# A two-layer graph network on one core: degrees counted in two halves inside the histogram, table rows begun there

## What is computed

```python
h = maximum(layernorm(x), 0)
# two graph convolutions over the edges plus one self loop per node
deg  = segment_sum(1, dst)                 # a count for each node, loop included
dinv = rsqrt(deg)
h = relu(segment_sum((h @ W)[src] * dinv[src] * dinv[dst], dst) + b)    # twice, W_pre ahead of W1
x = x + h @ W_post + b_post
h = maximum(layernorm(x), 0)
x = x + attention(h)                       # 4 heads; softmax over the heads; first N edges only
```

## Time and profile before

| | |
|---|---|
| median of 3 runs | 4163.26 us (4160.58 to 4163.69) |
| the profiled execution | 4164.72 us, its span 4163.0 us |
| busy | PE 3188.7 us (77%), DVE 1329.3 (32%), ACT 383.8 (9%), POOL 3026.6 (73%) |
| DMA | 514.10 MB, mean 123 GB/s |
| granted TensorE clock, mean | 0.825 |

### The profile page before, as it was taken

One profiled execution on the slowest core, in us unless ns is written; L12 is line 12 of the kernel. 1 busy time (PEld: TensorE's weight loads), 2 busy tenths in 40 slices (PEclk: granted clock), 3 DMA queues, 4 the chain that ended last, 5 costly groups with the idle time before them and its releaser, 6 DMA issues.

```text
span 4163.0 us, 38689 instructions
## 1 busy us (share of the span) xinstructions
PE 3188.7 (77%) x12023; PEld 1996.3 (48%) x12023; DVE 1329.3 (32%) x2800; ACT 383.8 (9%) x1055; POOL 3026.6 (73%) x3173
## 2 busy tenths in 40 slices
PE   5587787778788788787777777777777777777777
PEld 5344444444444444444444555544445555545566
DVE  6322222222222222222222333332224444434456
ACT  5100000000000000000001110111101111011112
POOL 2677777777777777777767777777777777777772
PEclk8677767777877877777778899999989899999987
DMA  7644444444444444444434444443334444444455
GB/s 228 153 121 116 121 115 121 118 118 121 116 121 118 118 121 115 121 118 119 121 99 120 118 118 121 118 118 111 113 115 118 118 118 118 118 121 126 119 163 153
DMA packets 248749, 514.10 MB, mean 123 GB/s; under 512 B 62491, under 2 KB 141832, under 8 KB 248296
## 3 DMA queue, kind: packets, MB, share of 16 engines
q0 software_dynamic: 150048, 410.73, 35.6%
q1 hardware_dynamic: 98504, 100.82, 8.3%
HBM read 471.70 MB, written 39.64 MB: 123 GB/s over the span
## 4 chain that ended last, share of the span: by engine, by line
POOL 67%; issue 22%; PE 5%; DMA 3%; DVE 1%; ACT 1%; POOLq 0%; SPq 0%; DVEq 0%
POOL sb_big L897 66%; DMA sb_big<-T,sb_srci 3%; PE bank L1181 3%; PE bank L541 1%; ACT sb_big L744 1%; PE bank L1658 0%; DMA T<-sb_big 0%; PE bank L1643 0%; POOLq L891 0%; DVE sb_big L1762 0%; PE bank L1107 0%; PE bank L1108 0%; DVE sb_big L791 0%; DVE sb_big L1709 0%; DMA sb_work<-dstT 0%
## 5 line engine op out<-in xcount | busy, mean ns | idle before, releaser
L897 POOL DMA_INDIRECT sb_big<-T,sb_srci x3126 | 2960.1, 947 | 982.5 <-issue 939.5
L1181 PE MATMUL bank<-sb_big 128*128 (+2 forms) x7056 | 2680.3, 490 | 862.2 <-DMA sb_big<-T,sb_srci 803.0
L1181 PEld LDWEIGHTS bank<-sb_big 128*128 128x128 f32 x7056 | 1382.2, 229 | 1908.6 <-issue 1759.6
L958 DVE TENSOR_TENSOR sb_work<-bank,sb_work 128x257 f32<-128x257 f32 (+1 forms) x196 | 83.4, 425 | 1609.2 <-PE bank L1181 1609.2
L945 DVE TENSOR_TENSOR sb_big<-bank,sb_win 128x2304 f32<-128x2304 f32 x196 | 501.2, 2557 | 6.7
L1011 ACT COPY sb_work<-bank 128x256 f32<-128x256 f32 x196 | 73.0, 373 | 1815.4 <-PE bank L1070 1815.4
L981 DVE SCALAR_TENSOR_TENSOR sb_work<-bank,sb_dinv,sb_b 128x256 f32<-128x256 f32 x98 | 47.4, 484 | 508.7 <-PE bank L1108 508.7
L991 DVE TENSOR_TENSOR sb_X<-sb_X,bank 128x256 f32<-128x256 f32 x98 | 41.2, 421 | 384.4 <-PE bank L1121 384.4
L1069 PE MATMUL bank<-sb_ident,sb_work 128*128 128x128 f32 x392 | 122.0, 311 | 20.3 <-DVE sb_work L981 14.3
L1070 PE MATMUL bank<-sb_ident,sb_work 128*128 128x128 f32 x392 | 120.5, 307 | 0.0
L1048 ACT COPY sb_work<-bank 128x256 f32<-128x256 f32 x98 | 36.5, 373 | 817.2 <-PE bank L1070 817.2
(11 more groups left out here) (192 smaller groups left out, 1712.5 us busy)
## 6 DMA issues: line engine op xcount, KB each, us to landing
sb_big<-T,sb_srci POOLq DMA_INDIRECT x3126, 2.8
T<-sb_big SPq DMA_DIRECT2D x14, 899.5 KB, 8.2
sb_work<-T SPq DMA_DIRECT2D x49, 257.0 KB
T<-sb_work SPq DMA_DIRECT2D x49, 256.0 KB, 2.3
sb_work<-T SPq DMA_DIRECT2D x49, 256.0 KB
sb_X<-x SPq DMA_DIRECT2D x13, 896.0 KB, 11.0
out<-sb_X SPq DMA_DIRECT2D x9, 1024.0 KB
sb_looks<-LO SPq DMA_DIRECT2D x23, 256.0 KB
```

Source lines behind the costliest of these rows:

```text
L897: pool.indirect_dma_start(out, None, table, bass.IndirectOffsetOnAxis(idx, 0)).then_inc(s.g[u % NSEM], 16)
L958: v.tensor_tensor(t.Y[:, b, 0:w], ps.A[b][:, 0:w], t.self[:, b, 0:w], ALU.add).then_inc(s.Y, 1)
L1181: mm = pe.matmul(ps.A[b][:, 0:w], t.S[:, b * K + k, :], rhs, start=(k == 0), stop=(k == K - 1))
```

## The change

It does six things. (1) The degrees are finished in two halves, tiles 0 to 62 and 63 to 97 (`HALF`): the first set of eight matmuls stands on PE behind chunk 3 (`HALF_CHUNK`), the second behind the histogram. (2) `dve_scales` of batch 0 and DVE's tiles of group 0 stand on DVE ahead of the last chunk of one-hot slices. (3) The statistics move: groups 3, 4, 5 lie between one-hot slices on DVE; ACT takes groups 7 and 8 from DVE as well, group 7 ahead of the table, group 8 between the table's groups 2 and 3, where ACT's last two evacuations stand too (`act_counted`). (4) The table has eight places for groups instead of six (`STAGES`): two in `sb_work`, six in `sb_big`, taken from its end; POOL and ACT wait ahead of group 3 for the whole histogram. (5) One-hot buffers lie elsewhere, with one of its own for the last chunk. (6) Since `sb_work` is needed early, the next destinations are loaded behind group 3 of x instead of behind all of x, and the count of unsorted ones moves from the check to the histogram (`dve_given`). Work of the same size is otherwise kept: 14 stores, 70 ACT tiles. The general path, which these inputs don't take, is adapted.

The core of the diff:

```diff
-ACT_STATS = (0, 1, 2, 6)
+ACT_STATS = (0, 1, 2, 6, 7, 8)
+HALF = 63
+HALF_CHUNK, COUNTED = 3, 3
+STAGES = 8
+STAGE_SLOT = (None, None, 36, 29, 22, 15, 8, 1)
...
+    staged, _ = take(work, 0, [2, GROUP * TW])
+    t.stage = [staged[:, k, :].rearrange("p (j d) -> p j d", d=TW) for k in range(2)]
+    t.stage += [t.ring[:, k:k + GROUP, :] for k in STAGE_SLOT[2:]]
...
         if g == 3:
...
+            sp.dma_start(t.dstn, a.dstN).then_inc(s.dstn, 16)
     sp.wait_ge(s.dve0, ZERO_X)
     sp.dma_start(t.X[0:LAST, NT - 1, :], a.x[(NT - 1) * P:N, :]).then_inc(s.x97, 16)
-    sp.dma_start(t.dstn, a.dstN).then_inc(s.dstn, 16)
...
+def pe_degrees(pe, t, s, ps, h):
+    c0, c1, out = degree_half(ps, h)
+    d = t.deg.rearrange("p (j q) -> p q j", q=8)
+    for q in range(8):
+        mm = pe.matmul(out, t.Eq[0:32, q, :], d[0:32, q, c0:c1], start=(q == 0), stop=(q == 7))
+    mm.then_inc(s.pe0, 1)
...
         if c < NOH - 1:
             mm.then_inc(s.hist, 1)
+        if c == HALF_CHUNK:
+            pe.wait_ge(s.eq, 16)
+            pe.wait_ge(s.odd, 2)
+            pe_degrees(pe, t, s, ps, 0)
     pe.wait_ge(s.odd, 4)
+    pe_degrees(pe, t, s, ps, 1)
...
-    act_stats(act, ch, t, s, 0)
-    act_stats(act, ch, t, s, 1)
+    for g in ACT_STATS[0:3]:
+        act_stats(act, ch, t, s, g)
+    ch.sync()
+    act.sem_inc(s.ast, 1)
     act.wait_ge(s.par, 16)
     act_evacuate(act, t, s, ps, 0)
-    act_stats(act, ch, t, s, 2)
...
+    for g in ACT_STATS[3:5]:
+        act_stats(act, ch, t, s, g)
+    act_evacuate(act, t, s, ps, 1)
+    act_table1(act, t, s, 0, ch, ps)
...
+        if r == 0 and g == COUNTED:
+            pool.wait_ge(s.hb, 4)
...
+def act_counted(act, ch, t, s, ps):
+    act_stats(act, ch, t, s, ACT_STATS[5])
+    ch.sync()
+    act.sem_inc(s.ast, 1)
+    act_evacuate(act, t, s, ps, 2)
+    act_evacuate(act, t, s, ps, 3)
...
+        if r == 0 and g == COUNTED:
+            act_counted(act, ch, t, s, ps)
...
         ins.then_inc(s.chunk, 1)
...
+        if c == 2:
+            dve_stats(v, t, s, 3)
+            dve_stats(v, t, s, 4)
+        elif c == 3:
+            dve_stats(v, t, s, 5)
+            dve_odd(v, t, s, ps, 0)
+        elif c == 4:
+            dve_given(v, ch, t, s)
+            dve_variance(v, ch, t, *BATCHES[0])
+            dve_sums(v, ch, t, s, 0)
+            dve_odd(v, t, s, ps, 1)
+            dve_degrees(v, ch, t, s, ps, 0)
+            dve_scales(v, ch, t, s, 0, 0)
+            dve_table1(v, ch, t, s, 0, 0, 1)
+    dve_table1(v, ch, t, s, 0, 1, 3)
     dve_stats(v, t, s, 9)
     ch.step(dve_stats(v, t, s, 10))
     dve_variance(v, ch, t, *BATCHES[1])
+    dve_odd(v, t, s, ps, 2)
+    dve_odd(v, t, s, ps, 3)
     dve_sums(v, ch, t, s, 1)
+    dve_table1(v, ch, t, s, 0, 3, 4)
+    dve_degrees(v, ch, t, s, ps, 1)
     dve_scales(v, ch, t, s, 1, 0)
-    dve_table1(v, ch, t, s, 0, 5, 8)
...
+    dve_table1(v, ch, t, s, 0, 4, 7)
     dve_stats(v, t, s, 11)
+    dve_table1(v, ch, t, s, 0, 7, 8)
     dve_stats(v, t, s, 12)
```

More of the change, by code:

```diff
@@ L218, in views @@
     o = 0
[L219 to L222, removed]
     t.zero, o = take(big, o, [544], BF16)
@@ L225, in views @@
     t.deg, o = take(big, o, [784])
+    v, o = take(big, o, [32 + 2 * HW, OHC], BF16)
+    w, last = take(big, o, [32 + 2 * HW, CHUNKS[NOH] - CHUNKS[NOH - 1]], BF16)
+    u, o = take(big, o, [32 + 2 * HW, OHC], BF16)
+    t.OH = [v, u] * (NOH // 2 - 1) + [v, w]
+    assert last <= STAGE_SLOT[2] * TW and (STAGE_SLOT[2] + GROUP) * TW <= RING * TW - SPILL
     t.bpx, _ = take(looks, 0, [2 * P])
@@ L254, in views @@
     t.row, o = take(big, o, [8, 100])
-    t.rowi, o = take(big, o, [100], I32)
+    t.rowi, _ = take(looks, 1000, [100], I32)
     assert o <= RING * TW + 2 * K * P, o
@@ L447, in semaphores @@
     s.x = [sem(f"x{g}") for g in range(NG)]
-    s.t1 = [sem(f"t1_{g}") for g in range(6)]
+    s.t1 = [sem(f"t1_{g}") for g in range(STAGES)]
     s.g = [sem(f"g{g}") for g in range(NSEM)]
@@ L501, in sp_heads @@
 def sp_heads(sp, t, s, a):
+    for k in range(2):
+        sp.wait_ge(s.t1[k], 16 * len(range(k, NG, STAGES)))
     sp.dma_start(t.attn[:, 0, :], bcast_rows(a.attn_r, P)).then_inc(s.heads, 16)
@@ L665, in dve_variance, with scaled @@
     ch.step(v.scalar_tensor_tensor(var, var, 1.0 / D, d, ALU.mult, ALU.add))
+def scaled(b, r):
+    c0, c1 = BATCHES[b]
+    degrees = {(0, 0): (0, HALF), (1, 0): (HALF, NT), (0, 1): (0, NT)}.get((b, r))
+    return degrees[0] if degrees else NT + c0, NT + c1, degrees
 def dve_scales(v, ch, t, s, b, r):
     c0, c1 = BATCHES[b]
-    lo, hi = (0 if b == 0 else NT + c0), NT + c1
+    lo, hi, degrees = scaled(b, r)
     v.scalar_tensor_tensor(t.rx[:, NT + c0:hi], t.var[:, c0:c1], EPS, t.rx[:, c0:c1],
@@ L691, in batch_of, with table1_stage, table1_rows @@
     return sum(1 for c0, c1 in BATCHES if c0 <= g * GROUP)
-def table1_slot(eng, s, g, r):
-    before = r * len(range(g % 6, NG, 6)) + g // 6
+def table1_stage(eng, t, s, g, r):
+    k = g % STAGES
+    before = r * len(range(k, NG, STAGES)) + g // STAGES
     if before:
[L698 to L704, removed]
+        eng.wait_ge(s.t1[k], 16 * before)
+    return t.stage[k]
+def table1_rows(eng, t, j, row, sync):
+    row = row[:, 0:D]
     sync(eng.tensor_scalar(row, t.X[:, j, :], t.mean[:, j:j + 1], 0.0, ALU.subtract, ALU.max))
@@ L756, in sp_table1, with dve_degrees, dve_given @@
             a.T1[g * GROUP * P:(g + 1) * GROUP * P, :].rearrange("(t p) d -> p t d", p=P),
-            t.ring[:, slot:slot + GROUP, :],
-        ).then_inc(s.t1[g % 6], 16)
+            t.stage[g % STAGES],
+        ).then_inc(s.t1[g % STAGES], 16)
 def wait_table1(eng, s, r):
-    for k in range(6):
-        eng.wait_ge(s.t1[k], 16 * (r + 1) * len(range(k, NG, 6)))
+    for k in range(STAGES):
+        eng.wait_ge(s.t1[k], 16 * (r + 1) * len(range(k, NG, STAGES)))
+def dve_degrees(v, ch, t, s, ps, h):
+    c0, c1, out = degree_half(ps, h)
+    v.wait_ge(s.pe0, (DEG_A, DEG_B)[h])
+    v.tensor_copy(t.degs[:, c0:c1], out)
+    ch.step(v.tensor_scalar(t.rx[:, c0:c1], out, 1.0, None, ALU.add))
+    if h:
+        v.sem_inc(s.dve1, 1)
+def dve_given(v, ch, t, s):
+    wb = t.wb[:, :].rearrange("p (i t) -> p t i", t=2)
+    v.tensor_scalar(wb, t.dsti[0:1, :, 0:NT // 2], 4, None, ALU.logical_shift_right)
+    v.wait_ge(s.pool0, DSTF)
+    v.wait_ge(s.pool0, DIFF)
+    ch.step(v.tensor_scalar(t.dstn, t.dstn, 0.0, None, ALU.max, ALU.add, accum_out=t.degs[:, NT:NT + 1]))
 def dve_begin(v, ch, t, s, ps):
     v.memset(t.zero, 0.0)
+    v.memset(t.rx[:, HALF:NT], 1.0)
     v.memset(t.onesr[:, :], 1.0)
```

82 lines of the change are left out of this document (25 added, 57 removed).

## The result

The changed kernel took 4159.18 us (median of 22 runs, 4153.31 to 4163.99), the kernel before 4166.15 (22 runs beside them, 4160.58 to 4170.03). The ratio is 0.9984, with 95% between 0.9977 and 0.999: 6.7 us faster, between 4 and 10. Its direction held, and the size lies inside the range, but under the border of 0.2%, on the side that the forecast had given 0.48 of its chances. The forecast took 0.2% as what a measurement of this kernel can't tell from none; with 22 runs beside 22 it can, since the interval leaves out 1.

The account below looks back on a forecast made before the run. The unchanged gathers bound the kernel, so only their start, set by the table's last store, could move. Scales, ACT's groups and the store train put that landing at 119.6 instead of 128.33: 4163.26 - 8.7 = 4154.6 us, range 4149 to 4161.

Parts of the forecast that it names:

- What bounds it: POOL's gathers stay unchanged; only their start at 129.3 us, released by the table's last store, moves, one for one.
- The first scales: From PE's chunk 3 through the first degrees to ACT's group 0, forecast at 56.1 us, 18.7 earlier than before.
- not shrinking: Upper bound for the first eight degree matmuls on PE: 3.7 us whatever the columns; 2.4 by columns, 3.0 taken.
- ACT from there: ACT's groups, group 8's statistics (6.71 us), evacuations (0.7) and batch 1's root summed from 56.1 to group 6 at 81.6.
- Chunk 5: Last one-hot slices on DVE ready at 61.2 to 65.6, PE done at 67.7 to 71.5; cost 0 to 0.7 us, taken 0.
- The rule of whole lengths: Such DVE and POOL instructions exclude each other for their whole length: at most four times 1.18 us in chunk 5.
- The start of the train: Group 4's store, behind batch 1's scales and DVE's tile, issued at 82.4 on an empty queue, landing at 88.0.
- The pace: Nine further stores at 3.51 us, mean of 3.39 (groups 0 to 9) and 3.62 (4 to 13): last landing 119.6.
- the rival of the later pace: Stores at 3.68 us apiece throughout, last landing 121.1, with small waits: 4156 to 4160 us; chance 0.33.
- as fast as loads: Rival: table stores at 351 GB/s, 2.62 us each, last landing 111.6, 16.7 us less, 4146.6; chance 0.03.
- Costs taken as zero: Added or moved work, such as next destinations, POOL's subtraction, second degrees, check and eight places, all priced at 0.
- The rival on the other side: Slower than before by 0.2%, if ACT's statistics of groups 6 and 7 end near 65 because x came late; chance 0.05.

Follow-up runs that it names:

- e4: The changed kernel with group 0's sums copied in place of ACT's statistics of group 8: 4157.96 us, ratio 0.9982 to the kernel before.
- e7: e4 with the last one-hot buffer's slices 96 columns apart instead of 86: one run, 4170.78 us beside 4176.62 of the kernel before.
- e1: The changed kernel with DVE's tiles of groups 4 and 5 ahead of the second degrees and batch 1's scales: 4155.09 us, ratio 0.9974 to the kernel before.
- e3: The changed kernel with first degrees, first scales and group 0 put back behind the whole histogram: 4175.72 us, ratio 1.0026 to the kernel before.
- e8: Stores alone, graph network left out, trains of 14: 48.8 and 47.9 us for rows of 257 floats, 39.1 for rows of 256.
- e13: Stores alone, trains of 14: 47.4 us for 1024-byte rows 1028 bytes apart, 40.3 for 1028-byte rows 1056, 1088 or 1280 apart.
- e2: The changed kernel with six places for groups instead of eight: 4155.61 us, ratio 0.9979 to the kernel before.
- e5: The changed kernel with each group stored twice, to a second table and to T1: one run, 4195.79 us.
- e9: e1 with the buffer spacing of e7 and group 8's statistics on DVE instead of ACT: 4160.31 us, ratio 0.9962 to the kernel before.
- e12: e9 with ACT's root of batch 1 ahead of group 5 instead of group 6: 4149.99 us, ratio 0.9963 to the kernel before.

## Why the prediction came out as it did

- **What bounds it.** Held. The gathers did not change, the time follows the first gather one for one, and that follows the last store.
- **The first scales.** PE came at 49.60 (forecast 49.3). The eight matmuls were sized wrong: 3.0 taken for 63 columns, 3.64 measured, at the bound "not shrinking" of 3.7. ACT's group 0 came at 56.88 instead of 56.1, 0.1 past the end of its range (56.8). Of the 0.8, 0.3 are PE's start and 0.64 the matmuls; the rest was a little quicker.
- **ACT from there.** Evacuations at 71.40 (forecast 70.5, both together 0.7 allowed), group 3 at 71.93 (71.2), root 79.59 (78.9), group 6 at 82.24 (81.6). The lateness of group 0 passed through at 0.6 to 0.9. The forecast added the statistics of group 8 as a term of its own, 6.7 us, and that was right in the sum. But they delay group 3 by only 1.5 us: the histogram ended at 69.95 (inside the forecast's 67.7 to 71.5), so without them ACT would have waited until 70.4 anyway, as e4 showed. Two limits stood 1.5 us apart, and the sum names one.
- **Chunk 5.** Its slices were ready at 62.4, inside the bounds (61.2 to 65.6). Three of POOL's four instructions ran beside them, from 58.21 to 61.64, and cost them little: 28 slices in 4.24 us are 151 ns each, against 121 for the last twelve of the kernel before with POOL idle, 0.9 us in all, and the longest took 397 ns. The rule of whole lengths that the prediction set beside its bound allowed 4.7 us; this stretch does not bear it out. The matmuls were not 60 ns each: the close buffer of part 5 of the change makes them 74 (e7). The forecast had listed the buffers and given their spacing no price. It costs 1.34 us on PE and nothing at the end as long as ACT's statistics last until 71.3; without them it is worth 1.6 us at group 3 (70.38 in e4, 68.77 in e7).
- **The start of the train.** Group 4's store at 83.0 (forecast 82.4), landed at 88.3 (88.0). The mechanism, DVE's tile behind the scales of batch 1 and a DMA gap before it, is shown by e1, which takes the wait away; the same rule gives e3.
- **The pace.** 3.56 taken from the run against 3.51: nine times that is 0.5 us. It lies between the two paces of before, nearer the later one, so the rival of the later pace was half right. What makes every train of this table slow is where rows start. With 1028 bytes from row to row a train takes 3.4 to 3.5 us a store with nothing beside it (e8, e13), and 2.8 to 2.9 with starts 1024, 1056, 1088 or 1280 bytes apart. That answers the rival "as fast as loads", which needed 2.62. The question left open in the prediction, why groups 4 to 13 came slower than groups 0 to 9, stays open: the rows start alike in both.
- **The end.** 0.3 for the start and 0.5 for the pace make the last landing 120.35 instead of 119.6, and the first gather 121.43 instead of 120.6: 7.9 us less for 8.7. In time it was 6.7 less (4 to 10), an interval that holds both. So nearly all of the miss in the first gather is the eight matmuls and the pace of the stores, the two terms taken between two bounds and not from a row of their own.
- **Costs taken as zero.** The next destinations: x was in time, and PE's chunk 3 ended when foreseen. POOL's subtraction at 20.31 slowed 16 slices of DVE from 2.50 to 5.84 us, 3.3 us where the forecast had 3.5 at worst, and none of it reached PE. The second degrees, 3.63 us, were ready at 76.8 and ACT asked at 79.6. The check was done at 107.2. The eight places: zero (e2).
- **The rival on the other side.** It did not occur. ACT's statistics ended at 47.1 (forecast 46.5) and ACT waited 0.9 us for bank 1, at 48.03. But e3 shows how near a loss lay by another way: without the early start the same edits are 11 us slower than before.

Not settled: why trains inside the kernel differ between 3.45 (e5) and 3.79 us a store (e9) from one execution to the next, and which late waits make up the 10 us over which single runs spread.

## What to carry to other kernels

Where a train of transfers sets the end, the start of its last unbroken stretch counts, not the first item: here 18 us of earlier start became 8, and 3.7 of the 10 lost went to the fifth group's small share on DVE, which stood behind scales that only the seventh needs (e1); statistics, spacing and root on ACT's way were worth another 4.1 (e9 and e12). Ask of each item which input it needs and put what needs less ahead; then move the next root or statistic into a wait that exists anyway. And where stores bound a stretch, look at the address at which each row starts before counting bytes.

## What the runs showed of the hardware

- Stores to HBM of 1024 or 1028 bytes a row: 47.4 to 48.8 us for 14 of 0.92 MB with starts 1028 bytes apart, 40.3 with starts 1056, 1088 or 1280 apart, 39.1 for 1024-byte rows without spaces (e8 and e13).
- fp32 matmuls over 32 partitions, the eight of one set of degrees: 3.63, 3.64 and 3.70 us (16 rows in the trace) at 35, 63 and 98 columns, all at a granted clock of 1.00 (2.4 GHz), so 227 to 231 ns each whatever the columns.
- bf16 matmuls of 24 columns: 74 ns where the slices lie 86 columns apart, 60 at 96 and at 158. The 255 matmuls took 16.78 us in all six kernels with 86, 15.44 in all three with 96.
- The same 16 slices on DVE: 2.50 us alone (from 15.30) and 5.84 beside a 3.63 us subtraction of POOL, 3.34 more, nearly POOL's whole length. One of the sixteen took 3575 ns, the median 232. Beside POOL's three instructions for the table at 58.21 to 61.64, 1.03 to 1.25 us each, no slice took more than 397 ns. The two rows, one behind the other on DVE, and the sixteen slices:

```profile
15.30 2.50 DVE L855 TENSOR_SCALAR sb_big<-sb_big 128x316 bf16<-128x316 bf16 x16
...
19.57 5.84 DVE L855 TENSOR_SCALAR sb_big<-sb_big 128x316 bf16<-128x316 bf16 x16
...
L855 DVE TENSOR_SCALAR sb_big<-sb_big x16: 228/232/3575, 19.6 to 25.2; 128x316 bf16<-128x316 bf16 x16
```

- PE's granted clock did not do the same in the two kernels. Before, PE's last matmuls ended at 72.8, and the window from 80 to 85 shows 0.50 (1.2 GHz), below; after, they ended at 80.0, and that window and all until 125 show 1.00 (2.4 GHz), though PE rested from 80.0 to 97.9 and again from 102.0 on. Of the two kernels that leave out the statistics of group 8, e4 shows 1.00 from 80 to 90 and e7 shows 0.50. It made no difference here: the four matmuls of the check took 2.07 us at 0.50 (before, from 107.42) and at 1.00 (after, from 97.91). Nothing tried explains it.

```profile
80.00:85.00 5.00, 0.00 (x0) 0.00 (x0) 4.89 (x16) 5.00 (x13) 4.79 (x5) 0.50 1.08 306
```
